# Attention: how probabilities and tokens are turned, and which engine makes high parts, value copies and divisions

## What is computed

```python
xn = _modulate(_layernorm(x, ln1_w, ln1_b), shift_a, scale_a)
q, k, v = (xn @ w + b split in 16 heads of 32)
attn = softmax(q @ k.T / sqrt(32)); out = attn @ v
x = x + (out @ wo + bo)
h = gelu(_modulate(_layernorm(x)) @ w1 + b1); x = x + (h @ w2 + b2)
```

## Time and profile before

| | us |
|---|---|
| median of 3 runs (2073.23 to 2078.99) | 2075.45 |
| profiled execution, span 2074.2 | 2075.99 |
| mlp stage | 0 to 765.8 |
| attention stage, from its first matmul to the next stage's first | 772.0 to 1356.8 |
| ffn stage | 1356.8 to 2074.2 |

### The profile page before, as it was taken

One profiled execution on the slowest core, in us unless ns is written; L12 is line 12 of the kernel. 1 busy time (PEld: TensorE's weight loads), 2 busy tenths in 40 slices (PEclk: granted clock), 3 DMA queues, 4 the chain that ended last, 5 costly groups with the idle time before them and its releaser, 6 DMA issues. The chain is left out here.

```text
span 2074.2 us, 32163 instructions
## 1 busy us (share of the span) xinstructions
PE 2015.1 (97%) x10706; PEld 1665.8 (80%) x10706; DVE 1304.5 (63%) x2302; ACT 672.2 (32%) x2006; POOL 367.6 (18%) x427
## 2 busy tenths in 40 slices
PE   6899999999999989999999999999999999999999
PEld 4678888887887878888888888778888788788887
DVE  6667776776776757888888888872534525244322
ACT  3222333322333224546464545541212212121111
POOL 4233333222222221111111111110101101010100
PEclk9999999999999999999999999999999999999999
DMA  8454444454444433232233232250210202111000
GB/s 299 151 172 161 153 148 136 157 173 154 154 150 137 152 125 82 81 84 79 81 81 86 71 91 71 82 173 14 69 52 31 78 5 82 37 46 66 16 21 21
DMA packets 162521, 208.41 MB, mean 100 GB/s; under 512 B 13100, under 2 KB 92552, under 8 KB 162440
## 3 DMA queue, kind: packets, MB, share of 16 engines
q1 hardware_dynamic: 150920, 173.17, 26.6%
q0 software_dynamic: 9360, 29.96, 4.9%
q10 hardware_dynamic: 2160, 4.20, 0.6%
HBM read 132.83 MB, written 57.67 MB: 92 GB/s over the span
## 5 line engine op out<-in xcount | busy, mean ns | idle before, releaser
L617 PE MATMUL mlp_y<-weights,mlp_h 128*128 128x512 f32 x1536 | 380.8, 398 | 11.8 <-DVE mlp_h L854 10.4
L617 PE MATMUL ffn_y<-weights,ffn_h 128*128 128x512 f32 x1536 | 377.4, 395 | 1.4 <-DVE ffn_h L854 1.4
L594 PE MATMUL mlp_m<-xn,weights 128*128 128x512 f32 x1536 | 371.1, 392 | 5.6 <-DVE xn L842 5.6
L594 PE MATMUL ffn_m<-xn,weights 128*128 128x512 f32 x1536 | 371.4, 391 | 4.7 <-PEq L145 2.8
L617 PEld LDWEIGHTS mlp_y<-weights,mlp_h 128*128 128x128 f32 x1536 | 288.8, 189 | 85.0 <-issue 9.0
L594 PEld LDWEIGHTS mlp_m<-xn,weights 128*128 128x128 f32 x1536 | 290.1, 189 | 69.6 <-DVE xn L842 6.0
L617 PEld LDWEIGHTS ffn_y<-weights,ffn_h 128*128 128x128 f32 x1536 | 288.2, 188 | 70.8 <-DVE ffn_h L854 2.3
L594 PEld LDWEIGHTS ffn_m<-xn,weights 128*128 128x128 f32 x1536 | 289.3, 188 | 68.6 <-issue 6.4
L852 DVE CAST ffn_h<-ffn_g 128x512 fp32r<-128x512 f32 x128 | 57.6, 450 | 377.9 <-ACT ffn_g L730 377.1
L730 ACT ACTIVATE ffn_g<-ffn_m,vecs 128x512 f32<-128x512 f32 x128 | 88.1, 688 | 553.9 <-PE ffn_m L594 553.9
L1220 PE MATMUL att_banks<-xn,weights 128*128 128x256 f32 x1536 | 197.2, 287 | 11.4 <-PEq L145 6.1
(11 more groups left out here) (130 smaller groups left out, 2079.6 us busy)
## 6 DMA issues: line engine op xcount, KB each, us to landing
x_tiles<-x SPq DMA_DIRECT2D x132, 256.0 KB, 2.9
x<-x_tiles SPq DMA_DIRECT2D x96, 256.0 KB, 3.1
mlp_bias<-gate_bias_rows POOLq DMA_DIRECT2D x64, 256.0 KB, 4.1
att_kdiag<-xn SPq DMA_DIRECT2D x128, 128.0 KB, 2.5
turned_squares<-mlp_xhat SPq DMA_DIRECT2D x62, 256.0 KB, 3.3
mlp_xmod<-turned_squares SPq DMA_DIRECT2D x62, 256.0 KB, 2.9
mlp_gate<-gate_rows SPq DMA_DIRECT2D x16, 768.0 KB, 6.1
x_tiles<-in_x_dram SPq DMA_DIRECT2D x32, 256.0 KB, 4.7
```

The costliest lines, as they stand in the source:

```text
L594: last = nc.tensor.matmul(m1_ps[:, c % 2, :], st.tiles[0](a, k, c), xn[:, parity, b, k, :], start=s == 0, stop=s == len(steps) - 1)
L617: last = nc.tensor.matmul(y_ps[:, tile, :], h[:, c % 2, a, tile * P:(tile + 1) * P], st.tiles[1](b, c), start=c == 0 and s == 0, stop=c == ...
```

## The change

In attention, TensorE no longer transposes. For probabilities: ACT writes the exponentials of a head in an order of 4 groups of 32 (reading every fourth column of the scores), DVE turns 32x32 squares of eight heads in one instruction, SP stores them to DRAM (512 KB) and loads them back in two DMAs in the order that completes the turn. For tokens: the way of the mlp stage, with the buffer `stage` shared between squares and weight pieces. ACT now makes the high parts of keys/queries, of x and of the attention output, the value copies, and the divisions of the last half of heads of the second row, one head at a time. GpSimd scales the maxima. The lists of all five engines are reordered, key/query products rotate over three PSUM banks, `project` of tile 0 writes to the first bank of the scores, and `weigh(row, 0)` moves into the next pair. The second pair is written out as well.

The diff, cut:

```diff
+            def store_squares(n, tile):
+                sp.wait_ge(squares_turned, swaps(n, tile) + 1)
+                sp.dma_start(sh.squares_dram[tile], stage[:, :]).then_inc(squares_stored, 16)
+            def load_squares(n, tile):
+                sp.wait_ge(squares_stored, 16 * (swaps(n, tile) + 1))
+                sp.dma_start(x[:, tile, :].rearrange("p (a m) -> p a m", a=NSQ),
...
+            def store_probs(row, tile, e):
+                sp.wait_ge(probs_turned, 2 * row + e + 1)
...
+            def load_probs(row, tile, e):
+                sp.wait_ge(probs_stored[e], 16 * (row + 1))
...
+                for u in range(2):
+                    sp.dma_start(probsT[e][:, u, :, :], half[u]).then_inc(probsT_loaded[e], 16)
...
# SP, one pair
+                load_x(n + 1, tile) for both tiles; store_probs(row - 1, 1, 0); load_residual(n - 1, 1); load_probs(row - 1, 1, 0)
+                diag(n, 0); store_probs(row - 1, 1, 1); load_probs(row - 1, 1, 1)
+                store_squares(n + 1, 0); store(n - 1, 0); load_squares(n + 1, 0); diag(n, 1)
+                load_residual(n, 0); store_squares(n + 1, 1); load_squares(n + 1, 1)
+                store_probs(row, 0, 0); load_probs(row, 0, 0); store_probs(row, 0, 1); load_probs(row, 0, 1); store(n - 1, 1)
# GpSimd
+                nc.gpsimd.tensor_scalar(negmax[:, heads], smax[:, heads], -scale, 1.0, ALU.mult, ALU.mult).then_inc(negmax_done, 1)
# TensorE, one pair
+                keys_queries(n, 1); keys_queries(n, 2); weigh(row - 2, 0)
+                for u in range(3, 2 * KC):
+                    if u == 6 and before:
+                        pe.wait_ge(exp_done, 2 * row - 1)
+                        project(row - 2, 0)
+                    pe.wait_ge(kq_ready, 2 * KC * n + u - 2)
                     keys_queries(n, u)
+                scores(n, 0, 0); scores(n, 0, 1); values(n, 0); weigh(row - 1, 1); values(n, 1)
+                scores(n, 1, 0); scores(n, 1, 1); project(row - 1, 1); first_keys(n + 1)
# ACT
+                    last = nc.scalar.activation(probs[:, e, :, at, :], s_ps[:, head, :].rearrange("p (i c) -> p c i", c=NSQ), ACT.Exp,
...
+                    last = nc.scalar.activation(probs[:, 1, :, at, :], probs[:, 1, :, at, :], ACT.Copy, scale=inv[:, head:head + 1])
# ACT, one pair
+                kq_high(n, 1); divide(row - 1, FIRST_HEADS); kq_high(n, 2); divide(row - 1, LAST_HEADS); out_high(row - 2)
+                kq_high(n, 3); kq_high(n, 4); kq_high(n, 5); (weight piece); kq_high(n, 6); kq_high(n, 7)
+                modulate(n + 1, 0); exponentials(row, 0, ALL_HEADS); exponentials(row, 1, ALL_HEADS)
+                copy_values(n, 0); out_high(row - 1); modulate(n + 1, 1); x_high(n + 1, 0); x_high(n + 1, 1); copy_values(n, 1)
+                exponentials(row + 1, 0, ALL_HEADS); exponentials(row + 1, 1, FIRST_HEADS)
+                kq_high(n + 1, 0); exponentials(row + 1, 1, LAST_HEADS)
# DVE
+                half = probs[:, e, :, :, :].rearrange("p c h i -> p (c h i)")
+                nc.vector.transpose(half, half).then_inc(probs_turned, 1)
# DVE, one pair
+                kq_low(n, 0); turn_probs(n - 1, 1, 0); kq_low(n, 1); invert(row - 1, 1); kq_low(n, 2); stats(n + 1, 0)
+                kq_low(n, 3); turn_probs(n - 1, 1, 1); out_low(row - 2); kq_low(n, 4); stats(n + 1, 1); kq_low(n, 5)
+                (weight piece); normalise(n + 1, 0); finish(row - 2, 0); kq_low(n, 6); kq_low(n, 7)
+                row_max(row, 0); row_max(row, 1); normalise(n + 1, 1); divide(row, 0); turn_probs(n, 0, 0)
+                out_low(row - 1); divide(row, 1); turn_probs(n, 0, 1); row_max(row + 1, 0)
+                x_low(n + 1, 0); x_low(n + 1, 1); row_max(row + 1, 1); finish(row - 1, 1); divide(row + 1, 0)
```

More of the change, by code:

```diff
@@ L1117, in is_next, with is_last, swaps @@
             return isinstance(n, int) and n >= NPAIR
+        def is_last(n):
+            return isinstance(n, int) and n == NPAIR - 1
+        def swaps(n, tile):
+            return TPP * (n - 1) + tile
         block = local.enter_context(nc.Block())
@@ L1221, in product @@
                 return last
[L1223 to L1229, removed]
             def keys_queries(n, u):
                 m, matrix = u % KC, (WK, WQ)[u // KC]
-                product(bank(5 - u % 2)[:, 0:PT], [(weight(a, matrix, k)[:, m * P:(m + 1) * P], xn[:, b, k, :])
-                                                   for k in range(KC) for a, b in MUL_HI_LO]).then_inc(kq_done, 1)
+                product(kq_bank(u)[:, 0:PT], [(weight(a, matrix, k)[:, m * P:(m + 1) * P], xn[:, b, k, :])
+                                              for k in range(KC) for a, b in MUL_HI_LO]).then_inc(kq_done, 1)
             def scores(n, tile, e):
@@ L1253, in values @@
             def values(n, tile):
[L1254 to L1265, removed]
+                pe.wait_ge(kq_ready, 2 * KC * n + (6, 7)[tile])
+                product(value_bank(tile), [(xn[:, a, k, tile * P:(tile + 1) * P], weight(b, WV, k))
+                                           for k in range(KC) for a, b in MUL_HI_LO]).then_inc(v_done, 1)
             def weigh(row, tile):
@@ L1380, in exponentials, with x_high @@
-            def exponentials(row):
-                for e in range(2):
+            def x_high(n, tile):
+                place = q if is_next(n) and n > NPAIR else xn
+                act.wait_ge(modulated, TPP * (n - 1) + tile + 1)
+                if is_next(n) and n > NPAIR:
+                    act.wait_ge(scores_done, 2 * B)
+                else:
+                    act.wait_ge(v_done, TPP * n)
+                nc.scalar.activation(place[:, HI, :, tile * P:(tile + 1) * P].rearrange("p k (a t) -> p k a t", a=NSQ),
+                                     xmod[:, tile, :, :, :].rearrange("p a k t -> p k a t"), ACT.Copy).then_inc(xhi_done, 1)
@@ L1383, in exponentials @@
                     if not is_first(row):
[L1384 to L1388 removed]
+                        act.wait_ge(probs_stored[e], 16 * row)
@@ L1390, in first @@
+            FIRST_HEADS, LAST_HEADS, ALL_HEADS = range(HALF // 2), range(HALF // 2, HALF), range(HALF)
             def first():
-                pass
+                kq_high(0, 0)
             def pair_step(n, before):
                 row = TPP * n
+                kq_high(n, 1)
                 if before:
-                    copy_probsT(row - 1, 1)
-                exponentials(row)
+                    divide(row - 1, FIRST_HEADS)
+                kq_high(n, 2)
+                if before:
+                    divide(row - 1, LAST_HEADS)
+                    out_high(row - 2)
+                kq_high(n, 3)
+                kq_high(n, 4)
+                kq_high(n, 5)
@@ new lines, in normalise, with x_low @@
+                dve.wait_ge(xhat_ready, swaps(n, tile) + 1)
+                nc.vector.transpose(stage[:, :], stage[:, :]).then_inc(squares_turned, 1)
+            def x_low(n, tile):
+                place = q if is_next(n) and n > NPAIR else xn
+                dve.wait_ge(xhi_done, swaps(n, tile) + 1)
+                hi, lo = (place[:, part, :, tile * P:(tile + 1) * P].rearrange("p k (a t) -> p k a t", a=NSQ) for part in (HI, LO))
+                nc.vector.tensor_tensor(lo, xmod[:, tile, :, :, :].rearrange("p a k t -> p k a t"), f32(hi), ALU.subtract).then_inc(xn_ready, 1)
```

399 lines of the change are left out of this document (235 added, 164 removed).

## The result

| | us |
|---|---|
| before, median of 4 (2073.23 to 2078.99) | 2075.27 |
| after, median of 4 (2142.31 to 2152.45) | 2144.72 |
| ratio, with its 95% interval | 1.034 [1.031, 1.037] |
| profiled execution of after, span 2150.7 | 2152.45 |

The change costs 69 us; the forecast was 2142. The profiled execution of after is the longest of its four, 7.7 us above the median. About 4 us of that lie ahead of attention: its mlp stage, in which no line was changed, ends that much later than in the profile of before (first matmul of attention at 776.24, against 771.98).

The account below looks back on a forecast made before the run. TensorE bounds attention before; after, a circle of waits without TensorE: 37.7 us plus 1.6 for strided exponentials, period 39.3. Fifteen periods add 58, head and tail 9, to 2076.0: 2143, against the median 2142; range 2055 to 2190.

Parts of the forecast that it names:

- (a): ACT: 16 exponentials of the odd row with accumulator reads, key high part 0 between; 5.9 us.
- (b): ACT high part 1, DVE low part 1, the reciprocal and handovers; 1.2 us.
- (c): ACT: 8 divisions at 0.4, high part 2, out_high and high part 3; 4.6 us.
- (d): DVE: low parts, transpose of last probabilities quarter, out_low, stats, weight piece, normalise, transpose of squares; 6.2 us.
- (e): SP: squares to DRAM and back, from issue of the store to the first modulate; 6.6 us.
- (f): ACT: modulate of tile 0, standing in front of the even row's exponentials; 1.6 us.
- (g): ACT: exponentials of the even row; 5.5 us.
- (h): ACT: value copy 0.5 and out_high of the row before 0.6; 1.1 us.
- (i): DVE: out_low, divide, transpose and row_max, ahead of the odd row's exponentials; 4.4 us.
- (j): GpSimd: scaling of the maximum 0.6 and a handover, before the odd row's exponentials; 0.65 us.
- TensorE as the bound: Attention: TensorE still decides, period 31 us, total 2019; chance 0.17 shared with outcomes up to a slightly shorter circle.
- Rival 3: Attention: new traffic holds up more than the squares' round trip; period 42 to 43 us, total 2180 to 2200; chance 0.15.

Follow-up runs that it names:

- the kernel with thin transfers: Against after, stores and loads of the probabilities carry a quarter of their bytes, output not the reference's; 2101.3 us.
- the last kernel: Tile 0's diagonal copies shared by GpSimd and SP, against the joined regrouping with out_low back ahead of the maximum; 2057.1 us, ratio to before 0.990.

## Why the prediction was right

**The mechanism.** The forecast was that pairs grow from 35.5 to 39.3 us though TensorE loses work, because a circle of ACT, DVE, SP and GpSimd steps takes longer than TensorE's stream. Measured 39.06 to 39.43, with TensorE idle before project 0, scores 1,1 and the first keys, and ACT before `modulate` and the odd row's exponentials, as listed under what would show it.

**The terms.** (a) 5.9: measured 5.85, at a slot of 0.342, where the earlier trace rows have 0.343 ((1091.42 - 1088.00) / 10, in the timeline above). (b) 1.2: 1.24. (c) 4.6: 3.65; four divisions take 1.28 with the tail, about 0.3 each, where I had 0.4 from the earlier trace rows. (d) 6.2: 6.35, the 1024-element turning at 1.25, priced at 1.22. (e) 6.6: 8.7 from the end of the turning to `modulate` (1065.60 to 1074.29). (f) 1.6: 1.56. (g) 5.5: 5.47. (h) 1.1: 1.18. (i) 4.4: 4.54. (j) 0.65: 0.60. Together 39.1.

**Two misses that cancel.** The exponentials' step of four elements in PSUM was to cost 1.6 us a pair. It costs nothing: the slot is 0.342 in both kernels. The rule of the Trainium skill in Vector Engine (DVE) Microarchitecture Reference, section Measured stream behaviour on trn2, speaks of DVE's ports, and this trace shows nothing like it for ACT reading PSUM. For DVE itself the rows bear out the direction and not the 0.65 cycle that the prediction quotes: 0.743 against 0.540 us is 0.40 ns an element, where 0.65 cycle at that page's 0.96 GHz would be 0.68 (an estimate). With the divisions (0.9 less) the sum would have been 36.8, and the time by it 2076 + 15 x 1.4 + 9 = 2106, just below the range that was called most likely. In its place stands 2.1 us more in (e). That the number came out within 3 us is luck in this part: a cost that does not exist stood in for one that was overlooked.

The step of the text that failed is "apart from (e) no transfer ends last, but the margins are 1 to 3 us". I had followed SP's list for whether its transfers arrive in time, not for when the squares' store itself is issued. Between the keys' low part and that store stand four diagonal issues, 2.62 us, and a store whose load waits 3.65 us for it; SP reaches the squares 1.9 us after DVE. With these numbers step (d) would have been overtaken by SP; the kernel with the divisions moved back shows that the difference isn't academic.

**DMA at load.** The share was forecast as 0.77 at 207 GB/s and was 0.66 at 208. The Trainium skill's figure in DMA: Bandwidth & Descriptors, section Latency and other measured facts, would have put up to 3.6 us on the two legs of (e). From issue to `modulate` they took 6.8 us (1067.47 to 1074.29), against 6.6 in the earlier trace rows, so the excess of (e) is the wait in front of the issue. That does not make load free: in the kernel with thin transfers, at a share of 0.47, the same two legs took 5.1 us, so three quarters of the probabilities' bytes cost some 1.6 us there, less than half of what that figure allows. The price of 6.6 was right for a reason that does not hold: the stretch of ffn that took 5.05 us was called the emptier one, but by the windows of before its share was 0.48 (1370.74 to 1375.79) and that of the mlp stretch 0.41 (529.89 to 536.51).

**Head and tail.** From the first exponentials of an odd row (808.93) to the last pair's (1400.33) are 15 periods of 39.43, so 15 x 4.0 = +60, where 58 was forecast. The head is 808.93 - 776.24 = 32.7, against 31 forecast. The tail is 1434.26 - 1400.33 = 33.9, against 31; in it both final projections run at 1.2 GHz, 5.23 us for 12 matmuls instead of 3.0. Head and tail give +13 instead of +9, the later start of the stage +4, ffn -1: 76.5 us between the two spans. The sum was made against the profiled execution of before and came to 2143; by the profiles it is 9 us short, by the medians 3.

**The rivals.** TensorE as the bound (2019) and with it the rule of the Trainium skill (Perfetto Trace Analysis, Identifying the Most-Contended Engine) to take the engine of highest occupancy first: the change did take 4 us a pair from it (busy 35.13 us in a pair of before, 31.29 in the short pair above), as the rule says, and lost 69 us. The rule was right about what could be had: once the circle is cut in the last kernel, TensorE is busy 94% of the stage and the time is below before. The period of 31 named there was not reached by any kernel; the best is 33.4. Rival 3 had the right place (the traffic holds up more) and for the larger part the wrong cause: what held up the squares' store was the order in one queue, and the lower clock was off the path.

## What to carry to other kernels

Write the list of every queue that issues DMAs into the sum like that of an engine: a load behind its own store holds everything queued after it for the store's whole landing time, here 3.7 us (it costs time only where nothing else ends later, as the first of the two stores showed), and it is read from that queue's waits, where a `store` that never waits for its producer is the sign of a late queue. When work leaves the bounding engine for others, walk the waits once around a period before counting loads. And when a circle is opened, look next for the idle spells that are left on TensorE: behind those of 1.8 and 2.7 us twelve products took 4.6 us instead of 3.0, behind those of 1.0 us they did not.

## What the runs showed of the hardware

- ACT reads 128 float32 out of PSUM with a step of four elements in the same slot as with step one (0.342 us with its accumulator read, medians of after and before). DVE's normalise with such a step took 0.74 instead of 0.54 in SBUF.
- DVE turns 32x32 squares of 1024 elements in 1.25 us, where 512 take 0.71. ACT's in-place scaling of 128 elements by a column (Copy) has a slot of about 0.3, below the 0.4 of the `modulate` form.
- A 512 KB store took 3.3 us from issue to landing at 208 GB/s and 3.6 at 243; a 128 KB one took 2.0.
- Diagonal copies of 128 KB took 3.0 us to land when SP issued them in after. In the last kernel, at a higher share, they took 3.8 from GpSimd and 4.3 from SP, so the issuer alone does not make them slower.
- GpSimd's scaling of 8 elements took 0.20 us in some places and 0.56 to 0.64 in others of the same pair. In after all 28 long ones overlap a DVE instruction with all its large operands in SBUF (normalise L1547, low part of x L1558), and the short ones lie beside DVE instructions that read PSUM or beside none, but for one that such an instruction touches at its edge. In the other runs too no long one lies elsewhere, though some short ones lie fully beside such an instruction. No run was made to try it.
